# Storing P first in the node stages, and issuing the next pass's first 16 gathers there

## The reference

```python
for l in range(3):                     # e is absent in the first layer
    parts = [x[src], x[dst]] + ([e] if l else [])
    e = relu(concat(parts) @ We[l] + be[l])            # per edge
    agg = segment_sum(e * edge_weight[:, None], dst)   # per node
    x = relu(concat([x, agg]) @ Wn[l] + bn[l])         # per node
```

## Time and profile before

| | us |
|---|---|
| median of 3 runs | 2162.61 (2161.85 to 2167.23) |
| the profiled execution | 2160.04 |
| its span, first to last instruction | 2158.2 |
| node stage "first" | 855.7 to 876.6 |
| edge pass 0 | 876.6 to 1262.5 |
| node stage 0 | 1262.8 to 1292.6 |
| edge pass 1 | 1292.6 to 1701.0 |
| node stage 1 | 1701.3 to 1730.4 |
| edge pass 2 | 1730.4 to 2119.3 |
| node stage 2 | 2119.6 to 2132.8 |

### The profile page before, as it was taken

One profiled execution on the slowest core, in us unless ns is written; L12 is line 12 of the kernel. 1 busy time (PEld: TensorE's weight loads), 2 busy tenths in 40 slices (PEclk: granted clock), 3 DMA queues, 4 the chain that ended last, 5 costly groups with the idle time before them and its releaser, 6 DMA issues. The chain is left out here.

```text
span 2158.2 us, 47819 instructions
## 1 busy us (share of the span) xinstructions
PE 1852.3 (86%) x14213; PEld 1425.3 (66%) x14213; DVE 1389.3 (64%) x4633; ACT 650.4 (30%) x1281; POOL 980.5 (45%) x1025
## 2 busy tenths in 40 slices
PE   5777689999999995588888867999999969999984
PEld 2332244545444443588888756999999769999983
DVE  8998621313232325588888854777777648888785
ACT  1379811212121212233333332333333411111121
POOL 2000067710000000477777725777777257777770
PEclk7888799999999996799999998999999979999998
DMA  3145700030000004455555525777777345555551
GB/s 101 44 94 110 115 8 3 2 5 0 0 0 0 0 0 159 156 152 155 154 151 153 151 82 156 228 224 224 224 226 224 114 123 152 155 151 151 153 148 36
DMA packets 193826, 242.14 MB, mean 112 GB/s; under 512 B 56452, under 2 KB 120223, under 8 KB 192975
## 3 DMA queue, kind: packets, MB, share of 16 engines
q1 hardware_dynamic: 161199, 172.73, 28.4%
q0 software_dynamic: 31840, 57.21, 11.2%
q10 hardware_dynamic: 576, 9.44, 1.1%
HBM read 149.76 MB, written 69.88 MB: 102 GB/s over the span
## 5 line engine op out<-in xcount | busy, mean ns | idle before, releaser
L1600 POOL DMA_INDIRECT rows<-p_dram,src_i x864 | 828.4, 959 | 337.1 <-issue 237.8
L1838 DVE TENSOR_TENSOR agg_t<-psum,agg_t 128x128 f32 x1380 | 391.1, 283 | 162.1 <-PE psum L1717 138.0
L975 PE MATMUL psum<-adj,parts 128*128 (+2 forms) x1750 | 339.7, 352 | 5.9 <-ACT agg L1054 4.4
L1771 ACT ACTIVATE rows<-rows 128x512 f32<-128x512 f32 x216 | 136.2, 630 | 578.7 <-DVE rows L1831 575.7
L1822 DVE TENSOR_SCALAR hot_w<-col_f,dst_loc,weight 128x128 f32<-128x128 f32 x864 | 303.2, 356 | 0.9
L975 PEld LDWEIGHTS psum<-adj,parts 128*128 128x128 f16 x1750 | 152.6, 97 | 191.8 <-issue 23.4
L1697 PE MATMUL psum<-w_c,before 128*128 128x128 f32 x1840 | 262.1, 287 | 0.0
L1682 PE MATMUL psum<-p_sb,pair_src 128*128 x1032 | 152.0, 294 | 119.2 <-DVE pair_dst L1812 67.2
L923 DVE SCALAR_TENSOR_TENSOR gate_room<-psum,b_h,gate_room 128x512 f32<-128x512 f32 (+1 forms) x35 | 23.9, 682 | 349.5 <-ACT gate_room L1061 349.5
L840 POOL DMA_INDIRECT records<-record_of,place_i x128 | 125.6, 981 | 266.0 <-issue 266.0
L1717 PE MATMUL psum<-hot_w,rows 128*128 128x128 f32 x1728 | 233.7, 280 | 0.0
(11 more groups left out here) (251 smaller groups left out, 2382.0 us busy)
## 6 DMA issues: line engine op xcount, KB each, us to landing
e_dram<-after SPq DMA_DIRECT2D x230, 256.0 KB
before<-e_dram SPq DMA_DIRECT2D x230, 256.0 KB
adj<-stage SPq DMA_DIRECT2D x196, 97.8 KB, 3.7
pair_rows<-sorted_rows SPq DMA_DIRECT2D x129, 128.0 KB
rows<-p_dram,src_i POOLq DMA_INDIRECT x864
hot_all<-dst_rows ACTq DMA_DIRECT2D x2, 3072.0 KB, 14.6
p_dram<-p_sb SPq DMA_DIRECT2D x6, 384.0 KB
records<-record_of,place_i POOLq DMA_INDIRECT x128, 2.1
```

The costliest lines, as they stand in the source:

```text
L975: mm = nc.tensor.matmul(psum[:, AGG_BANK, 0:n_cols], parts[:, w, part, :], adj[:, w, cols], start=(w == 0 and part == 0), stop=(w == WINDO ...
L1600: nc.gpsimd.indirect_dma_start(out=rows[:, b % ROWS, m * D:(m + 1) * D], out_offset=None, in_=p_dram, in_offset=bass.IndirectOffsetOnAxis( ...
L1771: nc.scalar.activation(e_of(q), source, ACT.Relu).then_inc(e_on, 1)
L1838: nc.vector.tensor_tensor(a, psum[:, A_BANKS[q % len(A_BANKS)], m * P:(m + 1) * P], a, ALU.add).then_inc(agg_on, 1)
```

## The change

In a node stage, all of P is made first, one window at a time with 128 columns, and stored in three DMAs of 8 windows and one for the last window; Q follows. DVE and ACT work on Q in groups of four windows instead of two. When the stores of P have landed, POOL issues the 16 gathers of the first four rest slots of the next pass, at the end of its stream in the node stage. `rows`, the ring, is therefore allocated for all passes. In the pass, POOL starts with the overflow tile and then rest slot 4.

The x half of the new x of the first five chunks (X_EARLY = 5) is issued by TensorE at the end of the edge pass, in the PSUM banks that come free there, and the node stage adds the agg half to it. In the stage "first", the turning of the sorted list stands after P, and its store after the stores of P.

```diff
+def gather_rows(nc, rows, t, p_dram, b, m):
+    s = b * QUAD + m
+    nc.gpsimd.indirect_dma_start(
+        out=rows[:, b % ROW_SLOTS, m * D:(m + 1) * D], out_offset=None, in_=p_dram,
+        in_offset=bass.IndirectOffsetOnAxis(ap=t["src_i"][:, s:s + 1].bitcast(U32), axis=0),
+    ).then_inc(t["rows_in"][b % ROW_SLOTS], 16)
...
+        STORES = ((0, 2), (2, 4), (4, 6))
...
-                sp.wait_ge(stored, 16 * len(starts))
+            if tables is not None:
+                sp.wait_ge(turned_on, 2)
...
+                sp.wait_ge(rows_out, 32)
...
             if products and update:
                 pool.wait_ge(updated, CHUNKS)
+            if products:
                 nc.gpsimd.memset(t["agg_t"][:], 0.0).then_inc(made, 1)
-            if tables is not None:
-                pool.wait_ge(tabs, 80)
+                if tables is not None:
+                    pool.wait_ge(tabs, 48)
+                pool.wait_ge(stored, 16 * (len(STORES) + 1))
+                for b in range(ROW_SLOTS):
+                    for m in range(QUAD):
+                        gather_rows(nc, t["rows"], t, p_dram, b, m)
...
-                o = psum[:, P_BANKS + c % U_BANKS, 0:n]
-                if c >= U_BANKS:
-                    pe.wait_ge(x_on, c - U_BANKS + 1)
-                nc.tensor.matmul(o, t["w_n"][:, 0, :], hT[:, c * CHUNK:c * CHUNK + n],
-                                 start=True, stop=False)
+                o = psum[:, c, 0:n]
+                if c >= X_EARLY:
+                    nc.tensor.matmul(o, t["w_n"][:, 0, :], hT[:, c * CHUNK:c * CHUNK + n],
+                                     start=True, stop=False)
                 nc.tensor.matmul(o, t["w_n"][:, 1, :], t["agg_t"][:, c * CHUNK:c * CHUNK + n],
                                  start=False, stop=True).then_inc(updated, 1)
...
+            if update:
+                for c in range(CHUNKS if not products else X_EARLY):
+                    new_x(c)
...
+            for g in groups:
+                if update:
+                    pe.wait_ge(x_on, g + 1)
+                product(p_bank(g), g, 0).then_inc(p_made, 1)
+                if update and g + X_EARLY < CHUNKS:
+                    new_x(g + X_EARLY)
...
+            for g in groups:
+                if not update:
+                    pe.wait_ge(p_out, g + 1)
+                elif g:
+                    pe.wait_ge(p_out, g)
+                product(q_bank(g), g, 1).then_inc(q_made, 1)
...
-            for b in range(REST_QUADS):
-                if b == 1:
-                    further_rows()
-                if b >= ROWS:
-                    pool.wait_ge(summed, slot_of(b - ROWS) + 1)
-                elif b >= 2:
-                    pool.wait_ge(spread, slot_of(b - 2))
+            further_rows()
+            for b in range(ROWS, REST_QUADS):
+                pool.wait_ge(summed, slot_of(b - ROWS) + 1)
                 for m in range(QUAD):
-                    if b >= ROWS and m == 2:
+                    if m == 2:
                         pool.wait_ge(spread, slot_of(b - ROWS) + 4)
...
+            pe.wait_ge(next_in, 16 * len(next_loads))
+            early_x(E_BANKS[(SLOTS - LAG - 1) % len(E_BANKS)])
             for q in range(SLOTS - LAG, SLOTS):
                 turn_and_sum(q)
-
+                early_x(E_BANKS[q % len(E_BANKS)])
+            for i, bank in enumerate(T_BANKS):
+                if e_after is not None:
+                    pe.wait_ge(after_on, SLOTS)
+                early_x(bank)
```

More of the change, by code:

```diff
@@ L58 @@
 ROW_SLOTS = 4
+X_EARLY = 5
 RECORD = 5
@@ L1313, in node_stage, with p_bank, q_bank, tiles @@
         turned_on = sem("turned_on")
-        pairs = [range(a, min(a + 2, WINDOWS)) for a in range(0, WINDOWS, 2)] if products else []
-        N = len(pairs)
+        groups = range(CHUNKS) if products else ()
         q_parts, p_sb = t["q_parts"], t["p_sb"]
[L1317 to L1321, removed]
+        BANKS, TURN_BANK = 8, 7
+        STORES = ((0, 2), (2, 4), (4, 6))
+        def p_bank(g):
+            return (g - 1) % BANKS if update else g
+        def q_bank(g):
+            return (g - 2) % BANKS if update else g
+        def tiles(g):
+            a = 4 * g
+            return a, len(group_tiles(g))
+        def sums(bank, k):
+            return psum[:, bank, 0:k * D].rearrange("p (k d) -> p k d", d=D)
         block = ctx.enter_context(nc.Block())
@@ L1359, in new_x, with product @@
                 n = chunk_width(c)
[L1360 to L1364 removed]
+                o = psum[:, c, 0:n]
+                if c >= X_EARLY:
+                    nc.tensor.matmul(o, t["w_n"][:, 0, :], hT[:, c * CHUNK:c * CHUNK + n],
+                                     start=True, stop=False)
                 nc.tensor.matmul(o, t["w_n"][:, 1, :], t["agg_t"][:, c * CHUNK:c * CHUNK + n],
                                  start=False, stop=True).then_inc(updated, 1)
+            def product(bank, g, half):
+                for k, w in enumerate(group_tiles(g)):
+                    mm = nc.tensor.matmul(psum[:, bank, k * D:(k + 1) * D], hT[:, w * P:(w + 1) * P],
+                                          t["w_ab"][:, half * D:(half + 1) * D], start=True, stop=True)
+                return mm
+            if update:
+                for c in range(CHUNKS if not products else X_EARLY):
+                    new_x(c)
+            if tables is not None:
+                pe.wait_ge(keep["first_in"], 48)
+            for g in groups:
[4 more added lines that the diff above has]
+                    new_x(g + X_EARLY)
             if tables is not None:
@@ L1371, in _ @@
                     for f in range(2):
-                        mm = nc.tensor.transpose(psum[0:n, P_BANKS + b, f * P:(f + 1) * P],
+                        mm = nc.tensor.transpose(psum[0:n, TURN_BANK, (2 * b + f) * P:(2 * b + f + 1) * P],
                                                  keep["sorted_in"][:, a:a + n, f], keep["ident"][:])
[L1374 to L1391, removed]
+                mm.then_inc(turned, 1)
@@ L1401, in second_part @@
[L1401 to L1404, removed]
+            def second_part(g):
+                a, k = tiles(g)
+                act.wait_ge(resid, g + 1)
+                nc.scalar.activation(q_parts[:, a:a + k, 1, :], residue[:, g % RESIDUES, 0:k, :],
                                      ACT.Copy).then_inc(mid, 1)
             if update:
-                for c in range(CHUNKS if not products else U_BANKS):
-                    take_x(c)
@@ L1410, in _ @@
[L1410 to L1419, removed]
+                for c in range(CHUNKS):
+                    n = chunk_width(c)
+                    act.wait_ge(updated, c + 1)
+                    nc.scalar.activation(hT[:, c * CHUNK:c * CHUNK + n], psum[:, c, 0:n],
+                                         ACT.Relu, bias=t["b_n"][:, 0:1]).then_inc(x_on, 1)
@@ L1421, in _, with third_part @@
+            for g in groups:
+                a, k = tiles(g)
+                act.wait_ge(q_made, g + 1)
+                nc.scalar.activation(q_parts[:, a:a + k, 0, :], sums(q_bank(g), k), ACT.Copy).then_inc(high, 1)
+                if g >= 1:
+                    second_part(g - 1)
+            if groups:
+                second_part(CHUNKS - 1)
         @block.vector
         def _(dve):
[L1423 to L1426, removed]
+            def third_part(g):
+                a, k = tiles(g)
+                dve.wait_ge(mid, g + 1)
+                nc.vector.tensor_tensor(q_parts[:, a:a + k, 2, :], residue[:, g % RESIDUES, 0:k, :],
@@ L1427, in third_part @@
                                         q_parts[:, a:a + k, 1, :], ALU.subtract).then_inc(low, 1)
             if tables is not None:
[L1430 to L1435, removed]
+                dve.wait_ge(keep["first_in"], 48)
@@ L1436, in _ @@
+            for g in groups:
+                a, k = tiles(g)
+                dve.wait_ge(p_made, g + 1)
+                nc.vector.tensor_tensor(p_sb[:, a:a + k, :], sums(p_bank(g), k),
+                                        t["b_rep_e"][:].unsqueeze(1).broadcast_to([P, k, D]),
+                                        ALU.add).then_inc(p_out, 1)
             if tables is not None:
@@ L1438, in _, with edge_pass @@
                 nc.vector.tensor_scalar(blocks, blocks, 7, None, ALU.logical_shift_right).then_inc(listing, 1)
[L1439 to L1457, removed]
+                dve.wait_ge(turned, 1)
+                for b, n in enumerate((P, SORT_TILES - P)):
+                    nc.vector.tensor_scalar(
+                        turned_rows[0:n, b, :, :],
+                        psum[0:n, TURN_BANK, 2 * b * P:2 * (b + 1) * P].rearrange("p (f l) -> p f l", f=2), 200.0,
+                        None, ALU.min).then_inc(turned_on, 1)
+            for g in groups:
+                a, k = tiles(g)
+                dve.wait_ge(high, g + 1)
+                if g >= RESIDUES:
+                    dve.wait_ge(low, g - RESIDUES + 1)
```

(7 more changed lines are left out.)

45 lines of the change are left out of this document (19 added, 26 removed).

## The result

The changed kernel takes 2193.61 us (median of 4 runs, 2192.81 to 2194.12) against 2164.39 for the kernel before beside it: ratio 1.0129, 95% interval 1.0107 to 1.0151. 2189 was forecast, with a range of 2176 to 2206. The profiled executions are 2160.04 us before and 2193.61 after, spans 2158.2 and 2191.7. The ratios of the experiments are against the runs of the kernel before that were made beside each of them (medians 2162.86 to 2166.44). One execution without the drain (4655.84 us) and one with a ring of 8 and no gathers (3116.05) took far longer than all others of their kernel, for a cause that was not found; the ratios leave them out.

The account below looks back on a forecast made before the run. POOL's gathers were taken to bound passes 0 and 2, TensorE pass 1. Stages and pass 0 summed as 14.5 - 2 + 9.7 + 10.9 - 5.0 = +28 us, 2188 on the profiled execution; 2189 was forecast, range 2176 to 2206.

Parts of the forecast that it names:

- The gathers hold the stage: End of each node stage with a next pass: block cannot end before POOL is through its 16 gathers, 20 us.
- the change doesn't hold the pass: Rival: the block's end does not wait for POOL, a stage ends with the work on Q; 2148 us, chance 0.03.
- 13 us uncovered per stage: Node stages with a next pass: P's landing plus gathers take 24 us, work on Q covers 11, leaving 13.
- 1 to 2 us before SP's first load: Sign in the first three node stages: the last gather stands 1 to 2 us before SP's first load of the pass.
- the sum of 28: Whole kernel: stage changes and the pass's gain, 14.5 - 2 + 9.7 + 10.9 - 5.0, add 28 us.
- The bounds: Limits on the time: 2180 below; 2203 above, with 2.7 us per stage for gathers to land and TensorE's lower clock.
- When P is out: Node stages: P lands 4.0 us after its last store's issue; passes 0, 1, 2 begin 14.5, 9.7, 10.9 us later.
- What the pass gets back: Edge passes: the four-slot ring makes slot 4 wait until 26 us; pass 0 gains 2 us, passes 1 and 2 nothing.
- the rival for both passes: Rival: POOL's chain shortens by all 16 gathers in passes 0 and 2, 20 us each; 2150 us, chance 0.05.
- The early half: Stage 2, without P or gathers: five x halves moved to the pass's end make it end 5.0 us earlier.
- The lower clock at a stage's start: TensorE may start a stage at the lower clock, 2.5 us in each of three; with landing about 2203, chance 0.15.
- The ports: Node stages: last steps of Q groups hold up gathers through a shared port pair, 15 us; 2203, chance 0.02.

## Why the prediction came out right

*The gathers hold the stage.* Right in size, wrong in the reason, and in that lucky. The step said that the block cannot end before POOL is through, as if POOL's stream held it, and gave "the change doesn't hold the pass" 0.03 and 2148 us. Without the drain POOL does hand in the end of the block ahead of its gathers, and the time is 2152.92. What stood between the two was the drain, an instruction of the block's end that no view counts as busy time. The evidence quoted for the step, POOL's start behind the barrier, fits both mechanisms.

*13 us uncovered per stage.* In stage 0 it is 14.7 (1300.24 to 1314.92), since the work on Q takes 9.8 us from the last P (1290.44) and not 11; that leaves the start of the pass where it was. The term that was too small is the end of the block. From the end of the last gather's row to the pass it takes 3.15 us (889.21 to 892.36), 3.5 and 3.15, not the 1.4 that the earlier trace rows gave for an end without gathers, and so the sign "1 to 2 us before SP's first load" did not hold. It makes 5.6 us in three stages, about the 6 us by which the sum of 28 missed the 34.1 of the trace; smaller misses of up to 1.5 us stand on both sides beside it. The bounds held it as landing, and the records of the drain bear that out in the main: in the three stages it ends 2.2 to 2.3 us after the last gather's row, and 0.70 us after the last landing of that gather (1316.47 in stage 0), and the block's end and the clearing block then take 0.9, 1.2 and 0.9 us. What the 0.70 us are stays open; behind 4 gathers they are 0.20.

*When P is out.* The first gather was forecast at 869.7, 14.0 us after the start of stage "first" (855.69), and found at 869.48, but 14.5 us after it (854.95): the time itself agrees by luck.

*What the pass gets back.* -2 was forecast for pass 0 and nothing for the others; with the tails that stand in the same row, -1.1, -0.3 and +2.4 came. The 26 us of the ring's rule were 25.8. The ring of 8 shows it from the other side: with slot 4 free at 14.8 us, 14.1 and 25.0 us come back, as the rival for both passes said it would from some 10 us on.

*The early half.* -5.0 at the end of stage 2 was forecast, and -6.0 came, with 2.4 us more in the pass before, -3.6 in all. In stages 0 and 1 it is worth 4.3 and 5.7 us with the gathers (45.3 to 41.0, 46.3 to 40.6) and 6.0 and 5.8 without them (30.1 to 24.1, 29.5 to 23.7).

*The lower clock at a stage's start* did not come in stages 0 to 2 (1.00 over the first 4 us of each), and the runs without the early half show that it filled the idle gap ahead of them. *The ports* did not either: the gathers beside the work on Q take 0.94 to 0.95 us in stage 0, 1.25 apart, like those behind it, and the last subtractions (L1450) 0.68 us, like those ahead of the gathers. (In stage "first" the first two take 1.00 and 0.96.) The rule that the prediction drew on costs nothing that these rows show. The Trainium skill, "SBUF — State Buffer", itself tells of a probe, in the section "Who interferes with whom", in which `tensor_tensor`, the kind of these subtractions, did not stall DMAs. The rows agree.

In all, by the medians: P first 0, early half -20, 16 gathers under a drain and a ring of 4 +48 us.

## What to carry to other kernels

Before work is moved ahead of a block's end, ask what that end waits for: here a drain of GpSimd turned 16 gathers, which the next pass could have run beside, into 17 us more of each stage. A lead is worth only what the next ring or wait lets through, so change both together or measure both (2193.61 as changed, 2158.38 with the ring, 2152.92 without the drain, 2117.06 with both). A short idle gap ahead of a stage, 3.93 us here, can cost TensorE's clock as well, and work that needs nothing late belongs into it.

## What the runs showed that I had not expected

GpSimd's sequencer comes to the end of a block with up to 12 gathers not yet begun, and passes it if no drain stands there. The Trainium skill, "Advanced Engine Details and Errata", in the section on the sequencer and the instruction queues, says that the sequencer pushes the engine's instructions into a queue, where they wait, and gives GpSimd's queue a depth of 8. The runs agree with the first and show 12 for gathers; what makes up the difference they don't show.

With 16 gathers, leaving out the drain makes passes 1 and 2 longer: by 3.6 us each with the ring of 4, and by 3.9 and 8.2 with the ring of 8. The overflow tile's row then stands behind all 16 gathers (issued at 1298.14, 14.3 us into the pass), and DVE waits 12.58 us for it. That this is the cause is argued from this wait alone and not shown: with 8 gathers pass 1 gets 2.1 us back and pass 2 loses 2.1.
